# ScalarE's gate multiply moved ahead of the Gelus, with four buffers for gated rows

## What is computed

```python
logits = xf @ Wr + br                                   # 4096 tokens, 8 experts
topv, _ = lax.top_k(logits, 2)
weights = softmax(where(logits >= topv[:, 1:2], logits, -inf))
h = gelu(einsum('td,edh->eth', xf, W1) + b1[:, None, :])      # 256 -> 1024
expert_out = einsum('eth,ehd->etd', h, W2) + b2[:, None, :]   # 1024 -> 256
out = einsum('etd,te->td', expert_out, weights)               # two experts a token
x = x + tanh(g_ffn[0]) * out
```

## Time and profile before

| | |
|---|---|
| median of 3 runs | 860.46 us (858.18 to 860.63) |
| profiled execution, its own time | 861.33 us |
| its span, first to last instruction | 859.6 us |
| mean granted TensorE clock | 0.968 |
| busy over the span: PE, DVE, ACT, POOL | 768.7, 581.4, 480.2, 349.0 us |

### The profile page before, as it was taken

One profiled execution on the slowest core, in us unless ns is written; L12 is line 12 of the kernel. 1 busy time (PEld: TensorE's weight loads), 2 busy tenths in 40 slices (PEclk: granted clock), 3 DMA queues, 4 the chain that ended last, 5 costly groups with the idle time before them and its releaser, 6 DMA issues. The chain is left out here.

```text
span 859.6 us, 27596 instructions
## 1 busy us (share of the span) xinstructions
PE 768.7 (89%) x8684; PEld 715.9 (83%) x8685; DVE 581.4 (68%) x1457; ACT 480.2 (56%) x1205; POOL 349.0 (41%) x390
## 2 busy tenths in 40 slices
PE   5499999999999999999827988999999999999992
PEld 3389889888898898888716987999999999999992
DVE  2358999989989999999863535655555555555551
ACT  2156566655656665556514536766666666666661
POOL 2234565555656555566540213333322233232222
PEclk9799999999999999999957999999999999999997
DMA  8876987777888888898245994543444333332222
GB/s 187 155 140 124 186 171 132 147 163 161 151 186 191 189 191 201 212 210 190 89 165 96 232 245 78 72 54 53 57 61 53 53 52 54 58 49 32 27 27 28
DMA packets 124028, 105.84 MB, mean 123 GB/s; under 512 B 60928, under 2 KB 117632, under 8 KB 121728
## 3 DMA queue, kind: packets, MB, share of 16 engines
q1 hardware_dynamic: 110032, 85.51, 46.9%
q0 software_dynamic: 13296, 18.23, 14.0%
q10 hardware_dynamic: 576, 0.56, 0.2%
HBM read 36.54 MB, written 32.19 MB: 80 GB/s over the span
## 5 line engine op out<-in xcount | busy, mean ns | idle before, releaser
L1290 ACT ACTIVATE hf<-bank,b1t,gscale 128x128 f32<-128x128 f32 x568 | 206.5, 468 | 130.3 <-PE bank L1412 127.9
L1265 POOL DMA_INDIRECT out_rows<-yg,gates x71 | 110.9, 1562 | 294.4 <-ACT yg L1299 229.4
L1412 PE MATMUL bank<-xh,wts 128*128 128x128 f16 x3408 | 204.1, 220 | 15.2 <-issue 15.2
L1412 PEld LDWEIGHTS bank<-xh,wts 128*128 x3408 | 198.4, 99 | 16.8 <-issue 15.2
L1426 PE MATMUL bank<-wts,hh 128*128 x1704 | 198.0, 273 | 6.0 <-DVE hh L1321 4.7
L1426 PEld LDWEIGHTS bank<-wts,hh 128*128 128x128 f16 x1704 | 163.5, 98 | 24.8 <-issue 7.1
L1320 DVE TENSOR_SCALAR hh<-hf,hscale 128x512 f16<-128x512 f32 x142 | 69.2, 487 | 168.0 <-ACT hf L1290 162.1
L540 POOL TENSOR_SCALAR_AFFINE_SELECT xh<-rowmax 128x512 bf16<-128x512 bf16 x128 | 93.7, 732 | 133.6 <-DVE rowmax L792 121.1
L1044 PE MATMUL bank<-va,probs 128*128 128x102 f32 x1024 | 138.9, 277 | 8.6 <-DVE ao L740 8.6
L1044 PEld LDWEIGHTS bank<-va,probs 128*128 128x128 f32 x1024 | 125.5, 192 | 11.6 <-DVE ao L740 6.2
L1321 DVE SCALAR_TENSOR_TENSOR hh<-hf,hscale,hh 128x512 f16<-128x512 f32 x142 | 106.7, 751 | 5.1
(11 more groups left out here) (169 smaller groups left out, 975.2 us busy)
## 6 DMA issues: line engine op xcount, KB each, us to landing
wts<-in_W SPq DMA_DIRECT2D x16, 1024.0 KB, 6.5
wts<-keys SPq DMA_DIRECT2D x96, 128.0 KB
wts<-queries SPq DMA_DIRECT2D x96, 128.0 KB
split_weights<-wts SPq DMA_DIRECT2D x8, 1024.0 KB, 5.1
wts<-split_weights SPq DMA_DIRECT2D x8, 1024.0 KB, 7.4
xin<-in_x SPq DMA_DIRECT2D x16, 256.0 KB, 2.8
cin<-in_ctx_in SPq DMA_DIRECT2D x16, 256.0 KB, 3.3
out_rows<-x SPq DMA_DIRECT2D x16, 256.0 KB
```

The costliest lines, as they stand in the source:

```text
L1265: pool.indirect_dma_start(out=out[:, :], out_offset=bass.IndirectOffsetOnAxis(ap=numbers, axis=0), in_=yg[m % 2][:, :], in_offset=None, co ...
L1290: last = act.activation(hf[b][:, c, :], HB[2 * b + half][:, c % 4 * TILE:(c % 4 + 1) * TILE], ACT.Gelu, bias=b1t[:, bass.ds(e, 1), c], sca ...
L1412: last = pe.matmul(HB[2 * b + half][:, c % 4 * TILE:(c % 4 + 1) * TILE], weight(expert[1], first_at(wp, k, c), P), xh[(m + 1) % RING][:, x ...
```

## The change

ScalarE's gate multiply of tile i - 1 moves from behind the Gelus of tile i + 1 to ahead of them, and `yg` gets four buffers instead of two, so that the multiply waits for the scatter four tiles before its own instead of two. GpSimd reads the buffer by the new number. Nothing else is touched.

```diff
-        yg = [sb(f"yg{i}", [P, D]) for i in range(2)]
+        yg = [sb(f"yg{i}", [P, D]) for i in range(4)]
...
-                            in_=yg[m % 2][:, :], in_offset=None, compute_op=ALU.add).then_inc(added, 16)
+                            in_=yg[m % 4][:, :], in_offset=None, compute_op=ALU.add).then_inc(added, 16)
...
                 def it(i, m, there):
+                    if there(-1):
+
+                        e, p = expert_of(act, i - 1), (m - 1) % 4
+                        act.wait_ge(yb_ready, i)
+                        when(act, before(i, 5), added, added_value(i - 5))
+                        act.activation(yg[p][:, :], yb[p % 2][:, :], ACT.Copy,
+                                       scale=gates[(m - 1) % RING][:, bass.ds(e, 1)]).then_inc(yg_ready, 1)
                     if there(1):
                         e = expert_of(act, i + 1)
                         b = (m + 1) % 2
...
                             last.then_inc(gelu_ready, 1)
-                    if there(-1):
-
-                        e, p = expert_of(act, i - 1), (m - 1) % 2
-                        act.wait_ge(yb_ready, i)
-                        when(act, before(i, 3), added, added_value(i - 3))
-                        act.activation(yg[p][:, :], yb[p][:, :], ACT.Copy,
-                                       scale=gates[(m - 1) % RING][:, bass.ds(e, 1)]).then_inc(yg_ready, 1)
```

## The result

The changed kernel takes 883.98 us in the median of four runs (882.87 to 885.07), where the kernel before took 860.55 (858.18 to 864.96, four runs): a ratio of 1.0245, 95% interval 1.0205 to 1.0284. The forecast was 878.5, slower, within 867 to 886. The profiled execution of the changed kernel took 882.87 us, its span 881.1.

A forecast was written before the change was run, and what follows sets the result against it. TensorE was taken to bound the expert loop at 5.30 us a tile; after the change a 5.65 us ScalarE-VectorE loop would. Start 469.93, 68 turns, 4.1 of stalls, 10.9 and 8.56 at the end gave span 877.7, median 878.5, range 867 to 886.

The forecast's parts named there:

- The bound before: Expert loop from tile 13 on: TensorE sets the pace, 5.30 us a tile, losing 4.7 us in waits for split `hh`.
- part 1: Four `yg` buffers: no gate multiply waits for a scatter in the slow stretch; gives back at most 4.7 us, and some end.
- M(8) against the landing of A(4): Tile 8's gate multiply, due at 514.4, against tile 4's scatter-add, landed by 513.8: tightest pair, 0.6 us to spare.
- the scatter rival: While last weights load: from 9.5 us a step scatters still block the gate multiply; 884 us, chance 0.04.
- Part 2, the loop: Gate multiply ahead of Gelus closes a ScalarE-VectorE chain without matmuls: 5.65 us a tile against TensorE's 5.30.
- Y to M: From the end of VectorE's `yb` write to the start of ScalarE's gate multiply: 0.11 us, ends 0.03 and 0.13.
- The stalls that lost their cover: Idle ahead of VectorE's `yb` write (2.3 us) and ScalarE's Gelus (1.8), now in the loop: 4.1 us, ends 0 and 8.
- The sum: Start at 469.93, 68 turns of 5.65, stalls 4.1, then the end: span 877.7, median 878.5 us, 2.1% slower.
- M to G: On ScalarE, from the gate multiply's start to the next Gelus' start: 0.74 us, 0.23 of it sequencer time.
- The sequencer that runs ahead: ScalarE's expert number loads while the gate multiply waits: loop 5.23 us, TensorE keeps the pace, 852 us; chance 0.12.
- About no change: ScalarE's sequencer runs ahead only in part: loop 5.41 us, 7.5 lost where 8.1 are regained, 860 us; chance 0.04.
- What would show it: Trace signs: Gelu starts 5.65 to 5.75 apart, TensorE about 94% busy, gate multiply waiting about 2 us for `yb`, not scatters.

The follow-up runs named there:

- the kernel with the number read first: Changed kernel, but ScalarE reads tile i+1's expert number ahead of the gate multiply's wait; ratio 0.9923 to the kernel before, median 858.03 us.

## Why the prediction was right, and where it was short

**The bound before, and part 1.** Right. With the buffers alone TensorE got back 49.51 - 44.23 = 5.3 us in the slow stretch, a little more than the 4.7 that were named. In the changed kernel no M waited for a scatter. The tightest pair was M(8) against the landing of A(4), as named; A(5) starts only when A(4) has landed:

```profile
514.04 1.65 POOL L1265 DMA_INDIRECT out_rows<-yg,gates  x1 [7.57 <-DMA out_rows<-yg,gates]
...
516.30 0.51 ACT L1287 ACTIVATE yg<-yb,gates 128x256 f32<-128x256 f32 x1 [2.03 <-DVE yb L1331]
```

The 0.6 us to spare became over 2: the scatters took (514.04 - 477.59) / 4 = 9.1 us a step from A(1) on where 9.4 had been taken, and M(8) came 0.5 us later behind A(1) than reckoned. The counterargument to the scatter rival, that the slow stretch ends by itself, was not what kept this pair apart: the first short step is the one after, from 514.04 to 519.32.

**Part 2, the loop.** Right in its parts: 1.64, 3.16, 0.13 and 0.75 against 1.64, 3.16, 0.11 and 0.74. Y to M came out at the upper end of its bounds. That 0.11 lay so near is in part luck: in the row behind it a scatter had come last, and not Y, as the prediction itself says. The low end, 0.03 from the earlier trace rows, did not apply to M, which has a register step between the wait and itself. For the Y that ended at 648.60 and the M that starts at 648.73, ScalarE's sequencer shows (durations in ns, first and last start):

```profile
L1287 ACTq FUSED_REGOPS  x1: 43/43/43, 648.6 to 648.6; - x1
...
L1229 ACTq TENSOR_LOAD <-tile_expert x1: 277/277/277, 648.7 to 648.7; - x1
```

In the kernel with the number read first, Y to M is 0.15.

**The stalls that lost their cover.** Right: 4.1 was taken; measured 861.63 - 471.37 = 390.26, less 68 x 5.68 = 386.2, leaves 4.0. Both named places show in the waits of the changed kernel: 3.1 us in 7 tiles ahead of Y, where 2.3 in 5 had been read before, and 17.4 us in 68 tiles ahead of G, which is 1.1 more than 68 x 0.24, where 1.8 had been reckoned.

**The sum.** The forecast was 5.5 us low, in these terms: the loop 390.26 instead of 388.3, 2.0; the start, G(2) at 471.37 instead of 469.93, 1.4, of which 1.0 is the first half of the program, whose first Gelu came at 461.39 instead of 460.41; the end, 872.26 - 861.63 = 10.6 to the last scatter instead of 10.9, and 8.8 behind it instead of 8.6, which cancel. The rest, 2.0, is that I took the median to lie 0.87 under the profiled execution, as before, where it lies 1.1 above. So the terms that were mis-sized are the length of a turn (0.02 in Y to M and 0.01 in M to G, in each of 68 turns) and what lies around the loop, which a single execution of before does not give better than a few us.

**The rivals.** The sequencer that runs ahead was rightly refused, for the reason given: the register step holds the wait, and the expert number's load stands behind it. The Trainium skill (Advanced Engine Details and Errata, Sequencer Loop) says that an engine instruction is pushed into its engine's queue and waits there for its semaphores. The rows of `k_rest` agree with it, those of M do not: the load of the expert number, which stands behind M, begins only with M's start, at 648.7, because M's register step, which is no engine instruction, comes first. But the rival's price for M to G was good: its 0.40 is the 0.41 that was measured once the number was read first. Its 0.03 for Y to M was not, so that loop is 5.33 and not 5.23, just over TensorE's 5.30 and not under it; by the ratio its time is 0.9923 x 860.55 = 853.9, beside the rival's 852. "About no change", a loop of 5.41, and the scatter rival did not appear.

**What would show it.** TensorE's share from 533 to 835 was 96% and not 94: the ends of matmuls in the record are modelled, and the last of a group reaches 0.16 us into the next group (640.89 + 2.78 = 643.67, where the next starts at 643.51), so that of the 0.38 us lost in a turn only 0.21 shows as idle in a typical one. The pace has to be read from start to start. The other signs (M to G with 0.24 idle, M waiting some 2 us in every tile, none for scatters) came as named.

## What to carry to other kernels

Before moving an instruction ahead of others on its engine, write down whether its input comes, through any engines, from the instructions that it is to precede one turn earlier; if so, the move closes a loop, and its length has to be added up and held against the busiest engine's time per turn, however idle the engines in it are. In such a loop the sequencer's own instructions (register loads, address computations, extra waits) lie in the sum as well: here a second read of the expert number cost 37 us inside the loop and nothing outside. To put such a read, or half of a long operation, outside of the loop was a small edit, and enough each time. Two edits that belong together in one change may pull in opposite directions: here the buffers alone gained 5 us and the order alone lost 27.

## What the runs showed of the hardware

I had expected TensorE's clock not to matter, and in the loop of the changed kernel it did not: the granted clock is 1.00 from 472 to 861 us. But after a stop of TensorE at the end of that kernel the next matmuls ran at half the clock. TensorE there, and the clock of the stretches:

```profile
859.01 2.78 PE L1426 MATMUL bank<-wts,hh 128*128 x24 [0.21 <-DVE hh L1321]
864.79 5.28 PE L1426 MATMUL bank<-wts,hh 128*128 x24 [2.99 <-DVE hh L1321]
```

```profile
858.00:861.70 3.70, 3.49 (x39) 2.90 (x36) 2.55 (x5) 1.43 (x5) 0.16 (x1) 1.00 0.35 42
861.70:864.70 3.00, 0.10 (x1) 0.00 (x0) 1.36 (x3) 2.84 (x8) 1.63 (x1) 0.85 0.15 8
864.70:870.20 5.50, 5.28 (x24) 3.42 (x24) 1.60 (x3) 0.51 (x1) 1.55 (x1) 0.50 0.19 26
```

The same 24 matmuls take 2.78 us at clock 1.00 (2.4 GHz) and 5.28 at 0.50 (1.2 GHz), after 2.99 us of idleness. In the kernel before they took 2.78 after 2.58:

```profile
518.75 2.78 PE L1426 MATMUL bank<-wts,hh 128*128 x24 [2.58 <-DVE hh L1321]
```

In the changed kernel it cost nothing that shows: the last multiply ended at 871.37, with the usual 0.82 to its scatter that is 872.19, and the scatter, which also waited for the one before it, started at 872.26. In the kernel with the new order alone, stops fall into the loop while it waits for scatters:

```profile
502.13 0.49 PE L1426 MATMUL bank<-wts,hh 128*128 x3 [1.10 <-DVE hh L1321]
503.78 4.09 PE L1426 MATMUL bank<-wts,hh 128*128 x21 [1.16 <-issue]
...
519.89 4.45 PE L1426 MATMUL bank<-wts,hh 128*128 x24 [3.24 <-DVE hh L1321]
```

After the stop of 3.24 us 24 matmuls took 4.45 instead of 2.78. Ahead of the 21 matmuls that took 4.09 there was no long stop, but two of 1.10 and 1.16 us with 3 matmuls between them. The mean granted clock of that kernel from 490 to 540 us is 0.93.
